# Pair attention in a four-layer vision tower: values projected per tile and moved by DMA to each image's rows, tables stored from GpSimd's queue

## The reference, cut to what matters

```python
qkv = x @ w_attn + b_attn                     # 256 -> 768
att = softmax(where(causal, q @ k.T / 4, -inf))   # per image and head, 37 x 37
y   = (att @ v) @ w_proj + b_proj
```

## Time and profile before

| | us |
|---|---|
| median of 3 runs | 1097.63 (1094.94 to 1102.04) |
| the profiled execution: its time | 1088.44 |
| its span, first to last instruction | 1086.6 |
| stage L0 attention | 36.9 to 146 |
| stage L2 attention | 482.5 to 592.5 |
| granted clock of TensorE, mean | 0.898 |

### The profile page before, as it was taken

How to read it: one execution, slowest core, us unless ns; L and a number is a source line. 1 busy time by engine, 2 the same in 40 slices (tenths; PEclk the granted TensorE clock), 3 DMA queues, 4 the chain that set the end, 5 groups by cost and what they waited for, 6 DMA issues and landing times. The chain is left out here.

```text
span 1086.6 us, 26178 instructions
## 1 busy us (share of the span) xinstructions
PE 905.5 (83%) x10336; PEld 671.7 (62%) x10336; DVE 607.6 (56%) x1308; ACT 527.9 (49%) x942; POOL 330.2 (30%) x425
## 2 busy tenths in 40 slices
PE   6889959499999789768997299999478898998666
PEld 6778726377777557557886144444267777777424
DVE  5475656766666279754663624222554564533476
ACT  3345547566566289634452155554123333443346
POOL 1211320445553000020313324442254453532102
PEclk9999968799999899869997599999788999998885
DMA  6200030200000100001012953222220000000001
GB/s 224 83 3 2 3 117 6 82 1 3 0 0 1 45 3 1 0 8 44 20 35 77 407 173 54 42 47 48 65 86 3 2 2 2 2 3 3 1 1 45
DMA packets 24307, 47.40 MB, mean 44 GB/s; under 512 B 4720, under 2 KB 15974, under 8 KB 23555
## 3 DMA queue, kind: packets, MB, share of 16 engines
q1 hardware_dynamic: 19859, 39.09, 10.4%
q0 software_dynamic: 4336, 6.74, 3.3%
HBM read 38.35 MB, written 7.47 MB: 42 GB/s over the span
## 5 line engine op out<-in xcount | busy, mean ns | idle before, releaser
L2755 PE MATMUL psum<-L2f_EW,weights_even 128*64 x176 | 81.7, 608 | 0.5 <-ACT weights_even L2454 0.2
L2756 PE MATMUL psum<-L2f_W,weights_even 128*64 128x512 f32 x176 | 81.7, 608 | 0.0
L2415 POOL DMA_INDIRECT expert_sums<-weights_even,L2f_target x20 | 35.0, 1750 | 76.1 <-DVE weights_even L2637 56.5
L1063 PE MATMUL psum<-L_cT,weights_odd 128*128 128x222 f32 (+1 forms) x192 | 45.1, 365 | 13.2 <-DVE L_by_sin L950 11.8
L2650 DVE TENSOR_TENSOR weights_even<-psum,weights_even 128x512 f32<-128x512 f32 x22 | 15.2, 692 | 72.2 <-PE psum L2756 70.2
L2274 PE MATMUL psum<-weights_even,L1f_H 128*111 128x256 f32 x176 | 46.8, 425 | 7.5 <-DVE L1f_H L2205 7.5
L425 ACT ACTIVATE L_PT<-psum 101x296 f32<-101x296 f32 x64 | 27.0, 421 | 49.1 <-PE psum L621 49.0
L882 ACT ACTIVATE L_U<-psum 128x592 f32<-128x592 f32 x32 | 21.2, 663 | 60.4 <-PE psum L1114 60.4
L2755 PEld LDWEIGHTS psum<-L2f_EW,weights_even 128*64 128x64 f32 x176 | 22.7, 139 | 43.2 <-issue 43.2
L2462 ACT ACTIVATE L2f_W<-L2f_EW 128x1024 f32 x44 | 46.3, 1053 | 6.2 <-PE psum L2756 5.6
L366 POOL TENSOR_TENSOR L_rs<-L_mv,ln_eps 111x2 f32<-111x2 f32 (+1 forms) x12 | 3.0, 252 | 146.0 <-DVE L_mv L518 139.3
(11 more groups left out here) (462 smaller groups left out, 2621.6 us busy)
## 6 DMA issues: line engine op xcount, KB each, us to landing
L2f_EW<-experts SPq DMA_DIRECT2D x24, 512.0 KB, 13.6
weights_even<-L_w SPq DMA_DIRECT2D x4, 1024.0 KB
patch_ring<-patches SPq DMA_DIRECT2D x11, 333.0 KB, 4.7
expert_sums<-L_blank SPq DMA_DIRECT2D x1, 1184.0 KB
weights_odd<-L_wo SPq DMA_DIRECT2D x1, 1024.0 KB
expert_rows<-X SPq DMA_DIRECT2D x5, 192.0 KB
expert_sums<-X SPq DMA_DIRECT2D x5, 192.0 KB
weights_even<-tok_w SPq DMA_DIRECT2D x3, 256.0 KB, 2.9
```

The lines of the kernel that those rows point to most:

```text
L1063: mm = nc.tensor.matmul(bank[:, h * NC2:h * NC2 + width(u)], wu[:, (2 * g + h) * 128:(2 * g + h + 1) * 128], cT[:, u % 2, n // 4, 0:width( ...
L2755: nc.tensor.matmul(core.bank(bank)[PAIR[0], :], xsT[:, j % 2, c, PAIR[0]], own, start=c == 0, stop=c == KD - 1)
L2756: mm = nc.tensor.matmul(core.bank(bank)[PAIR[1], :], xsT[:, j % 2, c, PAIR[1]], cols(W1[:, part], KD, NF)[:, c], start=c == 0, stop=c == K ...
```

## The change

For a unit, v_project(u) multiplies whole tiles: 111 columns of xT are the weights, all 256 value columns of wqkv move, two products for each tile. DVE adds the bias and writes by_tile, whose rows are a tile's (three images one below the other). Six DMAs from SP's queue for each unit (an image of each tile, by parity) copy 37 partitions at a time from by_tile to the partitions of V; a DMA takes both tiles, two runs of 544 bytes for each partition. The ones lie in by_tile and are moved along: a head has 17 columns instead of a pair's 34. values(s) waits for all six moves of its unit (v_moved).

The order changes: the values are projected in step B in the place of the keys, the keys in step C in the place of the first v phase; the second v phase, a part of step 0 too, is gone. k_out moves with the keys from ACT's step B to C. V's memset is one instruction, and neither PE nor DVE waits for it.

In L2 the first unit's moves stand in SP's program ahead of the blank store, the other units' behind it. The stores of unit rows into the two tables go from SP's to GpSimd's queue (copy_rows), after norm(u) and biased(u+2); the two short last stores stay on SP with semaphores of their own.

```diff
+                def move_values(u):
+                    images, n = UNITS[u][2], len(UNITS[u][1])
+                    sp.wait_ge(v_done, u + 1)
+                    after(sp, o_ps, pairs_of(u - 1))
+                    for i in range(min(PER, len(images))):
+                        for e in range(2):
+                            sp.dma_start(V[64 * e:64 * e + T, u % 2].rearrange("p (m i) e c -> p m i e c", m=2)[:, 0:n, i, e],
+                                         by_tile[i * T:(i + 1) * T, u % 2, 0:n, e]).then_inc(v_moved[u % 2], 16)
+
+                sp.wait_ge(zeroed, 2)
+                move_values(0)
                 if route:
                     sp.wait_ge(blank_set, 1)
                     sp.dma_start(core.dram["expert_sums"]...
-                    for u in range(NU - 1):
-                        sp.wait_ge(norm_done, u + 1)
...
+                for u in range(1, NU):
+                    move_values(u)
@@ ScalarE, a step
-                    if u + 1 < NU and s % 3 == 1:
+                    if u + 1 < NU and s % 3 == 2:
                         k_out(u + 1)
@@ VectorE
+                def v_out(u):
+                    n, rows = len(UNITS[u][1]), rows_of(u)
+                    dve.wait_ge(v_ps, u + 1)
+                    after(dve, v_moved[u % 2], moves(u - 2) if u >= 2 else 0)
+                    for m in range(n):
+                        last = nc.vector.tensor_tensor(by_tile[:rows, u % 2, m]..., core.bank(M1)[:rows, m * D:(m + 1) * D]..., bv..., ALU.add)
+                    last.then_inc(v_done, 1)
@@ TensorE
                 def k_project(u):
                     pe.wait_ge(xT_done, u + 1)
+                    after(pe, v_done, u + 1 if u else 0)
                     project(u, k_bank(u), D, k_ps)
+                def v_project(u):
+                    rows = rows_of(u)
+                    pe.wait_ge(xT_done, u + 1)
+                    for m in range(len(UNITS[u][1])):
                         for kd in range(KD):
+                            mm = nc.tensor.matmul(core.bank(M1)[:rows, m * D:(m + 1) * D], xT[:, u % 2, kd, m * R:m * R + rows],
+                                                  wqkv[:, kd, 2 * D:3 * D], start=kd == 0, stop=kd == KD - 1)
                     mm.then_inc(v_ps, 1)
@@ values(s)
-                    pe.wait_ge(v_done, v_phases(u + 1))
+                    pe.wait_ge(v_moved[u % 2], moves(u))
@@ TensorE, a step
-                        elif s % 3 == 1:
+                            v_project(u + 1)
+                        else:
                             k_project(u + 1)
-                        else:
-                            v_project(u + 1, 0)
...
-                    if u + 1 < NU and s % 3 == 2 and images_of(u + 1, 1):
-                        v_project(u + 1, 1)
```

More of the change, by code:

```diff
@@ L249 @@
 PR = 64 + T
[L252 to L260, removed]
 def pairs_of(units):
@@ L326, in at, with moves, rows_of @@
             return (img % IMGS) * T
+        v_moved = (even_moved, odd_moved)
+        def moves(u):
+            return 16 * sum(2 * min(PER, len(UNITS[v][2])) for v in range(u % 2, u + 1, 2))
+        def rows_of(u):
+            return R if len(UNITS[u][1]) == 2 else width(u)
         with nc.Block() as block:
@@ L346, in _ @@
                 nc.gpsimd.memset(P[:, :, :, T:64], 0.0).then_inc(zeroed, 1)
+                nc.gpsimd.memset(V[:], 0.0).then_inc(zeroed, 1)
                 if route:
                     nc.gpsimd.memset(blank[:], 0.0).then_inc(blank_set, 1)
[L349 to L354, removed]
                 pool.wait_ge(mine[0], mine[1])
@@ L380, in _ @@
                         biased(u + 2)
+                    if route and u < NU - 1:
+                        copy_rows(u)
                     if prep and u == 1:
@@ L390, in x_T @@
                     act.wait_ge(xT_ps, u + 1)
[L391 removed]
+                    after(act, v_ps, u - 1)
+                    after(act, k_ps, u - 1)
                     tiles = UNITS[u][1]
@@ L472, in _ @@
                 nc.vector.memset(core.bank(OB)[:PR, 0:272], 1.0).then_inc(set_up, 1)
+                nc.vector.memset(by_tile[:], 1.0)
+                dve.drain()
                 def shift(s):
@@ L491, in normalise @@
                     nc.vector.tensor_tensor(O[:PR, s % 2].rearrange("p c (e d) -> p c e d", e=2),
-                                            o[:, :, 0:32].rearrange("p c (e d) -> p c e d", e=2),
+                                            o[:, :, :, 0:16],
                                             r.unsqueeze(3).broadcast_to([PR, 8, 2, 16]), ALU.mult).then_inc(o_done, 1)
[L495 to L501, removed]
-                        src = core.bank(M2 if phase else M1)[rows, 0:k * 128].rearrange("p (i c d) -> p i c d", i=k, c=8)
-                        last = nc.vector.tensor_tensor(V[rows, u % 2, at0:at0 + k, :, 16 * e:16 * e + 16], src,
-                                                       cols(bv[rows], 8, 16).unsqueeze(1).broadcast_to([T, k, 8, 16]), ALU.add)
+                def v_out(u):
[3 more added lines that the diff above has]
+                    for m in range(n):
+                        last = nc.vector.tensor_tensor(by_tile[:rows, u % 2, m].rearrange("p e (c d) -> p e c d", d=17)[:, :, :, 0:16],
+                                                       core.bank(M1)[:rows, m * D:(m + 1) * D].rearrange("p (e c d) -> p e c d", e=2, c=8),
+                                                       bv[:rows].rearrange("p (e c d) -> p e c d", e=2, c=8), ALU.add)
                     last.then_inc(v_done, 1)
@@ L519, in residual @@
                     last.then_inc(var_ready, 1)
-                dve.wait_ge(zeroed, 2)
-                v_out(0, 0)
+                v_out(0)
+                dve.wait_ge(zeroed, 1)
                 for s in range(STEPS):
@@ L3117, in layouts @@
         out[f"{n}_bqk"] = column(g[bqkv][:2 * D])
-        out[f"{n}_bv"] = np.zeros((PR, 128), np.float32)
-        for e in range(2):
-            out[f"{n}_bv"][64 * e:64 * e + T] = g[bqkv][order][2 * D + 128 * e:2 * D + 128 * (e + 1)]
+        out[f"{n}_bv"] = row(g[bqkv][order][2 * D:])
         out[f"{n}_wo"], out[f"{n}_bo"] = kmajor(wo[by_pair], KD), row(g[bo])
```

70 lines of the change are left out of this document (31 added, 39 removed).

## The result

The change makes the kernel slower: 1146.86 us, median of 4 runs (1143.04 to 1151.52), beside 1097.74 of the kernel before; the ratio is 1.0447, with a 95% interval of [1.0404, 1.0490]. Every kernel here has some executions that are up to a few per cent slower, one of e11's far more, with a lower granted clock; the ranges show them, the ratios leave them out.

What follows compares the result with a forecast made beforehand. The prediction took PE's order, its work plus its waits, to bound the two changed stages. L0's 8.7 us and L2's 26.6 made 35.3 us, which on the median of the runs gave 1133 us, range 1112 to 1162.

Steps and rivals of the forecast that it cites:

- slow packets: Rival: the moves' packets take 42.7 ns each, so each wait for moves grows; 1166 us; chance 0.08.
- unit 0, steps 0 and 1: First unit of each stage: PE waits 6.7 us for moves at values(0); +3.6 us in L0, +4.0 in L2.
- blank store, values(3): L2: unit 1's moves queue behind the blank store on one engine, so PE waits 17.5 us at values(3).
- step B, three of +0.21: Value product replaces the keys' in step B: 0.29 us longer in units 1 to 3, +0.9 a stage.
- step C, four of +0.52 and unit 4's: Values wait for ACT's p_T copy behind k_out: 6.02 us against 5.47, +2.7 a stage.
- clock in the steps: Granted clock drops once after the long wait in each stage: +1.5 us in L0, +1.5 in L2.
- One engine for a move: A 37-partition move goes to one DMA engine: 25 ns a packet, 11.1 us for a unit's six moves.
- Tables on GpSimd: Four store issues a unit on GpSimd's queue, 2.2 us, cost nothing; at double that price 1.8 us once.
- Only the starts wait: Rival: moves share one engine but do not queue behind the blank store; 1114 us; chance 0.11.
- Moves spread or cheap: Rival: moves run on many engines and land in 3 us; 1099 us; chance 0.12.
- PE's work decides: Rival: moves land early and k_out's copy doesn't hold values in step C, which takes 4.2 us; 1082 us; chance 0.04.

Runs made afterwards that it cites:

- e11: The changed kernel itself, run again beside the kernel before: 1153.07 us, ratio 1.0520.
- e9: The changed kernel with the four table stores of copy_rows back on SP's queue, behind the moves: 1157.89 us, ratio 1.0593.
- e12: The changed kernel with the table stores back on SP's queue, once more, beside the changed kernel on one chip: 1155.84 us, ratio 1.0561.
- e1: The changed kernel with the blank store as 32 partitions of 37 rows: 1126.53 us, ratio 1.0234.
- e6: The changed kernel with spread blank store, moves split into 32 and 5 partitions, keys projected ahead of score(s) in step C, k_out first for ACT: 1108.63 us, ratio 1.0114.
- e7: The changed kernel with spread blank store, split moves, keys first in step C, and copy_rows on SP behind the moves: 1099.61 us, ratio 1.0066.
- e8: The changed kernel with spread store, split moves, keys first, copy_rows on SP, and unit 0's odd-head moves issued from GpSimd's queue: 1087.85 us, ratio 0.9961.
- e4: The changed kernel without moves: V set to ones, values(s) waiting for v_out alone: 1105.48 us, ratio 1.0007.

## Why the prediction was right or wrong

The sign and the waits held: 1133 forecast, in a range of 1112 to 1162, 1146.86 measured. The sum of 35.3 us was too small; the medians differ by 49.1, the profiled stages by 61.7. The measured time lies just above the 1124 to 1145 that the prediction gave its own sum, and inside the range only because that was widened for slow packets, which did not come; that part of the hit is luck. Term by term, from the step table (the clock is what is left of the differences when the other terms are taken out):

| term | L0 forecast | L0 | L2 forecast | L2 |
|---|---|---|---|---|
| unit 0, steps 0 and 1 | 3.6 | 5.2 | 4.0 | 5.5 |
| blank store, values(3) | - | - | 17.5 | 14.4 |
| step B, three of +0.21 | 0.9 | 0.6 | 0.9 | 0.6 |
| step C, four of +0.52 and unit 4's | 2.7 | 2.8 | 2.7 | 2.8 |
| clock in the steps | 1.5 | 14.4 | 1.5 | 10.6 |
| behind the last step | 0 | -0.6 | 0 | 6.9 |
| ahead of step 0 | 0 | -1.7 | 0 | 0 |
| sum, before rounding | 8.7 | 20.8 | 26.6 | 40.9 |

- **One engine for a move: right.** Share 0.07 with 22 GB/s while the moves run alone. 544 bytes at 22 GB/s are 24.7 ns a packet, 444 of them 11.0 us; forecast 25 and 11.1. The Trainium skill's rule ("DMA: Bandwidth & Descriptors", section "Why a DMA increments its semaphore by 16 and not by 1") agrees with this trace for 37 as it did for 74, 101 and 111. The price by the same page's "Why small descriptors are slow (HBM only)", 8.9 us by my estimate in the prediction, does not: the moves took the time that the small loads showed.
- **Unit 0: right, 1.5 us short.** The waits are 8.19 and 8.17 us for 6.7. From the first issue to PE's release six moves take 14.7 us in both stages (44.71 to 59.38, 514.97 to 529.63) where 13.3 were forecast: the packets were right, what comes on top of them was too small.
- **The blank store: right in place and cause, 3 us too long.** Its share of 0.14 ends near 552, 21.2 us after score(2) at 530.79, and values(3) is let go at 566.89, 36.1 after score(2). The forecast had 24.3 and 542.5 - 506.9 = 35.6. That the sums meet is luck: the store was through 3.1 us sooner, and unit 1's moves behind it took 14.9 us instead of 11.3. GpSimd's stores among them are 1.0 us of that by e9 and e12; the rest stays open. The wait is shorter since PE came later: at 552.46, 21.7 after score(2) and not 18.1, because steps C and A before it ran at the lower clock. e1 shows the cause by removing it. The saving there, 21 to 29 thousandths (23 to 31 us) by the two ratios of the changed kernel, is more than the wait: in the profiles L2 is 24.3 us shorter, 15.0 in that step, 5.2 in the steps behind it and 4.2 after the last.
- **Step C: right to 0.03 us.** 5.99 for 6.02, with ACT's copy as the releaser, the same wait as unit 0's in the earlier trace rows. That unit 0 was the one place where PE waits held for L2 alone: in L0 step C of unit 1 waited 1.30 us for DVE (after 1.21).
- **The clock: the term that was mis-sized.** The prediction said of the drop in the earlier trace rows: "The waits of about 7 us in L0 and of 17.5 in L2 are new and longer gaps; I charge one such drop each, +1.5 and +1.5." It charged for the long waits and put the short one that it had itself found, in every step C, at nothing. The runs show that nearly all steps A behind it run at 0.55 to 0.72, 1.3 to 2.9 us longer each, and that filling the wait puts all of them back to 4.82. These are 7.3 us in L0 and 6.9 in L2. Steps C of units 0 and 1 add 0.3 to 2.4 us each beyond the step's own 0.5, and unit 4's steps in L0 another 4.6; in all it comes to 14.4 and 10.6 us in the profiled stages, for 1.5 and 1.5. The rows of before could not have given the size: there a wait of 1.45 us in unit 0 was followed by a step of 6.96 in L2 and one of 5.48 in L0, and the 1.30 us of L0 by no drop. e11, with 3 us less of it in L2's steps and 4 less behind them, shows that the size varies from execution to execution.
- **Tables on GpSimd: mis-sized as well.** Forecast nothing, bound 1.8. The four issues take 2.56 us and are not over when L2's last norm is due, and behind them the norm stands 1.61 us (1.70 in e6) between two of its instructions; where GpSimd issues nothing ahead of them (e7, e9, before) they follow after 0.15 us. After, from norm to last norm:

```profile
645.57 2.44 POOL L372 TENSOR_SCALAR X<-L_z,L_mv,L_rs 111x256 f32<-111x256 f32 x2 [0.18 <-issue]
648.31 1.34 POOL L381 DMA_DIRECT2D expert_rows<-X  x2 [0.30 <-POOL X L372]
...
652.77 0.58 POOL L369 TENSOR_TENSOR L_rs<-L_rs,minus_half 111x1 f32<-111x1 f32 x1 [1.61 <-issue]
653.53 1.23 POOL L372 TENSOR_SCALAR X<-L_z,L_mv,L_rs 111x256 f32<-111x256 f32 x1 [0.18 <-issue]
```

  7.96 us; before it was 6.20. So some 2 us at that point, inside the 6.9 behind the last step. The rest of the 6.9 goes with a clock of 0.60 there (before 0.81); that it is the clock's is not shown by a run of its own.
- **The rivals.** "Only the starts wait" is what e1 makes true: 1.0234, 1123 on the base of the medians, where the rival had 1114; e1's steps A are together 8.1 us longer than before, about the 9 between them. "Moves spread or cheap" had 1099, and e4 without moves came to 1098 by its ratio. For "PE's work decides" (1082) both of its conditions had to be built, in e6 and e8; together they gave 1087.85 beside 1092.61, 0.4% faster where the rival had 1.4%. "Slow packets" fell with the 24.7 ns.

What stays open: how much of the whole time the filling gives back beside the changed kernel on one chip; whether the tables' queue matters to the whole; and what beyond a gap sets whether and how far the clock falls behind it.

## What to carry to other kernels

Here a DMA's partition count decided how many engines carried it. 37 partitions had one, and a 1.2 MB store of 74 partitions on that same engine held a 39 KB move, and PE behind it, for 14 us; re-cutting the store to 32 partitions (share 0.86) was the cheapest gain of the study.

Price a short wait of PE by the steps after it, not by its own length: 1.3 us in each step C went with up to 2.9 us in the step behind it, in 41 of 48 cases. Look in a profile for a step with the same instructions and no idle bracket that has become longer, and read its clock. One profile isn't enough for its size: the same kernel had 7 us less of it in its second.

When work moves to another step, ask which engine's fixed order stands between it and the next need; here k_out lost the o_project that had hidden it, and the remedy that worked in part (e6) was to project the keys first and to put k_out first in ACT's step.

## What was not expected of the hardware

- Splitting a copy inside SBUF into more engines' worth of DMAs moves the bound to the queue that issues them: 0.75 us for each on SP, 12.06 us for 16.
- A queue whose engine is backed up holds the issuing engine as well. Behind the blank store one move's issue kept SP for 22.99 us in the changed kernel, and for 3.28 us in e1, where the store was spread:

```profile
524.37 1.89 SPq L343 DMA_DIRECT2D expert_sums<-L_blank  x1
526.30 22.99 SPq L336 DMA_DIRECT2D L_V<-L_by_tile  x1
```

- GpSimd paid for its DMAs twice at L2's last norm: 0.61 to 0.67 us for each issue (1.22 and 1.34 for two), and 1.6 to 1.7 us ahead of the second compute instruction behind them.
- Matrix products whose result is thrown away made the steps after them up to 2.9 us shorter, and their own no more than 0.3 longer.
